# Three edits in one: a bias matmul over 128 rows instead of 3, the second layer norm's statistics on ScalarE, a cast written as a maximum

## The reference, cut to what matters

```python
x = x + linear_attention(layernorm(x)) @ W_proj + b_proj   # 16 heads of 8, causal running sums
z = layernorm(x)                    # (x - mean) / sqrt(var + 1e-5), over 128 channels
logits = z @ Wr + br                # 8 experts
# the two best experts of each token, their softmax weights normed to sum 1
h = relu(z @ W1[e] + b1[e])         # 512 wide
y_e = h @ W2[e] + b2[e]
x = x + sum of weight_e * y_e over the token's two experts
```

## Time and profile before

| | us |
|---|---|
| median of 3 runs | 402.93 (401.96 to 403.1) |
| the profiled execution, time | 401.86 |
| the same, span of the profile | 400.1 |
| PE busy | 311.0 (78%) |
| DVE busy | 297.5 (74%) |
| POOL busy | 280.4 (70%) |
| ACT busy | 193.4 (48%) |
| mean granted TensorE clock | 0.894 of full speed |

### The profile page before, as it was taken

The page is one execution under the profiler, slowest core; times in us unless marked ns, Lnnn a source line. Parts: engine busy times, 40 slices in busy tenths (PEclk is TensorE's granted clock), DMA queues, the critical chain, the costliest instruction groups (busy, mean ns, idle before and its releaser), DMA issues.

```text
span 400.1 us, 8377 instructions
## 1 busy us (share of the span) xinstructions
PE 311.0 (78%) x2477; PEld 241.8 (60%) x2477; DVE 297.5 (74%) x702; ACT 193.4 (48%) x480; POOL 280.4 (70%) x251
## 2 busy tenths in 40 slices
PE   5899999696979959889841389998999999993000
PEld 4678766464646636666530368887888888882000
DVE  6898998996779898799963777766666667773067
ACT  2788216557223210533312256776677777771072
POOL 3869376899457887887765636878788788787500
PEclk9999999899899987999955569999999999998555
DMA  7970000000000100000110142312423233111198
GB/s 221 346 221 1 2 0 0 2 2 0 2 0 20 35 28 20 27 22 27 41 48 33 47 128 70 81 56 87 115 83 83 83 91 89 43 43 52 46 374 256
DMA packets 23958, 29.26 MB, mean 73 GB/s; under 512 B 3806, under 2 KB 18569, under 8 KB 23916
## 3 DMA queue, kind: packets, MB, share of 16 engines
q1 hardware_dynamic: 18934, 19.02, 15.9%
q0 software_dynamic: 4544, 9.38, 7.3%
q10 hardware_dynamic: 438, 0.33, 0.3%
HBM read 16.04 MB, written 12.67 MB: 72 GB/s over the span
## 4 chain that ended last, share of the span: by engine, by line
PE 32%; DVE 23%; issue 19%; POOL 13%; ACT 9%; DMA 3%; SPq 0%; POOLq 0%; DVEq 0%; ACTq 0%
POOL y_rows L514 9%; PE ps L1191 7%; DVE work L845 4%; PE ps L1190 3%; DVE nd L851 3%; POOL x_rows L479 3%; DVE y_s L862 3%; PE ps L1162 2%; PE ps L1392 2%; ACT xs L610 2%; DVE x L1123 2%; PE ps L1362 2%; PE ps L1393 2%; PE ps L1364 2%; PE ps L1363 2%
## 5 line engine op out<-in xcount | busy, mean ns | idle before, releaser
L514 POOL DMA_INDIRECT y_rows<-kvt,yid x78 | 95.5, 1225 | 30.3 <-issue 21.0
L479 POOL DMA_INDIRECT x_rows<-rows,pos_i x64 | 66.1, 1034 | 30.2 <-issue 17.3
L449 POOL TENSOR_TENSOR kvt<-qk,v 128x1024 f32<-128x1024 f32 x32 | 67.6, 2136 | 24.4 <-PE ps L1195 13.2
L1191 PE MATMUL ps<-kvt,tri 128*128 128x384 f32 (+1 forms) x192 | 70.2, 477 | 12.1 <-DVE work L845 12.1
L676 ACT ACTIVATE wraw<-ps,b1s 128x256 f32<-128x256 f32 x156 | 61.3, 475 | 2.8 <-PE ps L1364 2.5
L1191 PEld LDWEIGHTS ps<-kvt,tri 128*128 128x128 f32 x192 | 37.0, 200 | 33.0 <-issue 16.5
L1071 DVE CAST wraw<-wraw 128x1024 f16<-128x1024 f32 x39 | 27.2, 696 | 34.7 <-ACT wraw L676 33.4
L1075 DVE TENSOR_TENSOR wraw<-wraw 128x1024 f16<-128x1024 f32 x39 | 47.8, 1226 | 1.3
L845 DVE TENSOR_TENSOR work<-ps,qk 128x1152 f32<-128x1152 f32 x32 | 42.2, 1351 | 3.5 <-PE ps L1195 3.2
L1362 PE MATMUL ps<-wraw,w1h 128*128 128x256 f16 x156 | 43.4, 278 | 0.3 <-issue 0.3
L1363 PE MATMUL ps<-wraw,w1h 128*128 128x256 f16 x156 | 43.3, 278 | 0.0
(11 more groups left out here) (211 smaller groups left out, 650.0 us busy)
## 6 DMA issues: line engine op xcount, KB each, us to landing
wraw<-x_rows SPq DMA_DIRECT2D x39, 130.0 KB, 2.6
qk<-y_rows SPq DMA_DIRECT2D x8, 512.0 KB, 6.6
wraw<-in_L_ffn_W_dram SPq DMA_DIRECT2D x1, 2048.0 KB, 11.8
out_dram<-x SPq DMA_DIRECT2D x8, 256.0 KB, 4.5
x<-in_L_attn_x_dram SPq DMA_DIRECT2D x3, 512.0 KB, 7.9
y_rows<-kvt,yid POOLq DMA_INDIRECT x78, 2.5
x_rows<-empty SPq DMA_DIRECT2D x9, 130.0 KB, 3.1
x_rows<-rows,pos_i POOLq DMA_INDIRECT x64, 2.3
```

The source lines that it names most:

```text
L449: nc.gpsimd.tensor_tensor(kvt[:, u % RING, a].rearrange("p (j h i) -> p j h i", j=DH, i=DH), k.unsqueeze(1).broadcast_to([P, DH, H, DH]), ...
L479: nc.gpsimd.indirect_dma_start(out=x_rows, out_offset=bass.IndirectOffsetOnAxis(ap=pos_i[:, c, t:t + 1], axis=0), in_=rows[:, t, :], in_of ...
L514: nc.gpsimd.indirect_dma_start(out=y_rows, in_=ysb[:, n % YG, g], in_offset=None, out_offset=bass.IndirectOffsetOnAxis(ap=yid[:, n, g:g + ...
L1191: nc.tensor.matmul(o, tri[:, :], kv[a][:, cols], start=(a == 0), stop=True)
```

## The change

The bias matmul of the experts' output reads 128 rows: the tile b2p has 128 partitions, set to zero on GpSimd, of which the first three take the pieces; the weights are the 128x128 ones that the first stage has already. `copy_x2` on ScalarE becomes two activations that also give each row's sum. A new `statistics` on ScalarE, for unit s - 1 and between `copy_yT(s)` and `copy_x2(s)`, turns the sums into negative means and takes squares of x minus mean with their sum (the squares themselves go to a place that is written again later). GpSimd's `layer_norm_2` gets one more small operation, which turns the sum of squares into the variance. VectorE's `statistics` and `moments_2` go. The high half is the maximum of the fp32 tile with itself, written in fp16.

```diff
-        b2p = sb("b2p", [3, E, D], BF16)
-        ones3 = sb("ones3", [3, P], BF16)
+        b2p = sb("b2p", [P, E, D], BF16)
@@ SP
+            sp.wait_ge(late_done, 16)
-            sp.dma_start(b2p[:, :, :], b2_parts).then_inc(b2_in, 16)
+            sp.dma_start(b2p[0:3, :, :], b2_parts).then_inc(b2_in, 16)
@@ GpSimd
-            nc.gpsimd.memset(ones3[:], 1.0).then_inc(late_done, 1)
+            nc.gpsimd.memset(b2p[:, :, :], 0.0).then_inc(late_done, 1)
@@ layer_norm_2(g), GpSimd
-                pool.wait_ge(stats2_done, g + 1)
-                nc.gpsimd.tensor_tensor(rstd[:, 1, gt], lnt[:, 4, gt], neghalf[:, gt], ALU.pow).then_inc(rstd2_done, 1)
+                pool.wait_ge(squares_done, G_LAST[g] + 1)
+                nc.gpsimd.tensor_scalar(var[:, gt], squares[:, gt], 1.0 / (D * X_SCALE ** 2), LN_EPS / X_SCALE ** 2, ALU.mult,
+                                        ALU.add).then_inc(var_done, 1)
+                pool.wait_ge(var_done, g + 1)
+                nc.gpsimd.tensor_tensor(rstd[:, 1, gt], var[:, gt], neghalf[:, gt], ALU.pow).then_inc(rstd2_done, 1)
@@ ScalarE
             def copy_x2(u):
                 act.wait_ge(proj_done, u + 1)
-                nc.scalar.activation(tiles(x, u), ps[:, 7, 0:T].rearrange("p (a d) -> p a d", a=TPU), ACT.Copy).then_inc(x2_done, 1)
+                for a in range(TPU):
+                    t = u * TPU + a
+                    ins = nc.scalar.activation(x[:, t], ps[:, 7, a * P:(a + 1) * P], ACT.Copy, accum_out=sums[:, t:t + 1])
+                ins.then_inc(x2_done, 1)
+            def statistics(u):
+                act.wait_ge(x2_done, u + 1)
+                nc.scalar.activation(tiles(mean, u), tiles(sums, u), ACT.Copy, scale=-1.0 / D).then_inc(mean_done, 1)
+                act.wait_ge(mean_done, u + 1)
+                for a in range(TPU):
+                    t = u * TPU + a
+                    ins = nc.scalar.activation(rows[:, t, 0:D], x[:, t], ACT.Square, bias=mean[:, t:t + 1],
+                                               accum_out=squares[:, t:t + 1])
+                ins.then_inc(squares_done, 1)
@@ ScalarE, step s
                 copy_yT(s)
+                if s >= 1:
+                    statistics(s - 1)
                 copy_x2(s)
@@ VectorE, step s
-                if s >= 1:
-                    statistics(s - 1)
...
-                if s - 1 in ended_by:
-                    moments_2(ended_by[s - 1])
@@ hidden_high(n), VectorE
-                nc.vector.tensor_copy(hh[:, n % 2], hid[:, n % 2]).then_inc(hi_done, 1)
+                nc.vector.tensor_tensor(hh[:, n % 2], hid[:, n % 2], hid[:, n % 2], ALU.max).then_inc(hi_done, 1)
@@ down(n), TensorE
-                nc.tensor.matmul(both, ones3[:, :], b2p[:, bass.ds(e, 1), :].broadcast_to([3, GPB, D]), start=True, stop=False)
+                nc.tensor.matmul(both, ones_b[:, :], b2p[:, bass.ds(e, 1), :].broadcast_to([P, GPB, D]), start=True, stop=False)
```

More of the change, by code:

```diff
@@ L145, in block_kernel @@
         lnt = sb("lnt", [P, 7, NT])
+        sums = sb("sums", [P, NT])
+        mean = sb("mean", [P, NT])
+        squares = sb("squares", [P, NT])
+        var = sb("var", [P, NT])
         rstd = sb("rstd", [P, 2, NT])
@@ L258, in block_kernel @@
         x2_done = sem("x2_done")
-        bn2_done = sem("bn2_done")
-        stats2_done = sem("stats2_done")
+        mean_done = sem("mean_done")
+        squares_done = sem("squares_done")
+        var_done = sem("var_done")
         rstd2_done = sem("rstd2_done")
@@ L466, in layer_norm_2 @@
                 gt = tiles_of(g)
-                pool.wait_ge(stats2_done, g + 1)
-                nc.gpsimd.tensor_tensor(rstd[:, 1, gt], lnt[:, 4, gt], neghalf[:, gt], ALU.pow).then_inc(rstd2_done, 1)
+                pool.wait_ge(squares_done, G_LAST[g] + 1)
[3 more added lines that the diff above has]
+                nc.gpsimd.tensor_tensor(rstd[:, 1, gt], var[:, gt], neghalf[:, gt], ALU.pow).then_inc(rstd2_done, 1)
                 pool.wait_ge(rstd2_done, g + 1)
-                nc.gpsimd.tensor_tensor(shift[:, 1, gt], lnt[:, 3, gt], rstd[:, 1, gt], ALU.mult).then_inc(shift2_done, 1)
+                nc.gpsimd.tensor_tensor(shift[:, 1, gt], mean[:, gt], rstd[:, 1, gt], ALU.mult).then_inc(shift2_done, 1)
             def scatter_x(n):
@@ L647, in _ @@
                     norm_2(ended_by[s - 2])
+            statistics(U - 1)
             for g in (NG - 2, NG - 1):
@@ L863, in quotient @@
                                         rd[:, par].unsqueeze(2).broadcast_to([P, TPU, DH, H]), ALU.mult).then_inc(y_done, 1)
[L865 to L875, removed]
             def split_low(g):
@@ L1035, in foreign_slots @@
                 link(nc.vector.tensor_tensor(aside[:, :, :], outside[:, 0], spare[:, :, :], ALU.mult))
-            statistics(U - 1)
-            moments_2(NG - 1)
             choose(FIRST)
```

## The result

The changed kernel took 398.0 us (median of 12 runs, 396.45 to 399.42) against 402.81 for the kernel before (12 runs, 400.38 to 403.4): ratio 0.9888, 95% interval 0.9866 to 0.991. The forecast was 398.6. The profiled execution took 398.36 us, span 396.6, mean granted clock 0.889.

What follows compares the result with a forecast made beforehand. No single engine was taken to decide; in the expert blocks TensorE sets the pace, then a fixed tail. The terms -4.4 + 0 - 4.7 + 4.5 + 0.3 = -4.3 gave 397.6 us profiled, 398.6 as median, range 395.5 to 402.

Steps and rivals of the forecast that it cites:

- Part 1: Expert blocks: bias matmul over 128 rows saves 0.20 us a block on TensorE, -4.4 us (0 to -5.5).
- rival A: Bias matmul: the chip sees no gap from its rows, so -4.4 goes and time is 403.0 us; chance 0.13.
- a fixed tail: End of the expert blocks: after VectorE's last subtract frees GpSimd, what remains was taken as fixed.
- Part 2: Expert blocks: the cast as a maximum adds 0.53 us a block on VectorE but costs 0 (-1 to +2).
- Rivals C and D: Scatters: C, two-input operations don't hold them, 387.7 us, chance 0.05; D, GpSimd can't get between maximum and subtract, 428, 0.03.
- covered: Blocks 1 to 6: VectorE is some 1.5 us late in total, but the stall of block 12 hides it.
- Part 3: Attention steps: statistics moved to ScalarE; VectorE -4.7, ScalarE +4.5, GpSimd's extra operation +0.3 us.
- ScalarE's term: Attention: +0.9 us from yT copy to next denominator, counting in steps 2, 4, 5, 6 and 11: +4.5 us.
- Rival B: Attention: a sum output costs 0.4 and nothing overlaps, 2.15 us a step instead of 0.9; 407.3 us; chance 0.11.
- VectorE's relief: Attention: VectorE loses two bn_stats per step and seven small operations per group, -4.7 us (-2 to -6).
- the four terms of 0.95: Attention steps 6, 9, 11 and 13: VectorE's small group operations leave the path before the next multiply, 4 x 0.95 us.
- the bounds of part 3: Attention: VectorE's saving -2 to -6 us, ScalarE's cost +1.8 to +8.5; named as the source of the forecast's range.

Runs made afterwards that it cites:

- the 64 rows: Kernel before with only the bias matmul changed, to 64 rows instead of 3, on a chip where the kernel before takes 401.83 us: 400.84 us, ratio 0.9984.

## Why the prediction was right, point by point

**Part 1, -4.4: right in mechanism; right in size partly by luck, since the sum of it is made up otherwise.** The gap was 0.20 a block as predicted and went in full; rival A is refuted by the bias alone and by the 64 rows. But blocks came to 3.03, not 2.99. PE in one of the longer blocks of the changed kernel:

```profile
291.28 0.22 PE L1399 MATMUL ps<-w,wraw 128*128 x1
291.34 0.22 PE L1400 MATMUL ps<-w,wraw 128*128 x1
291.46 0.23 PE L1399 MATMUL ps<-w,wraw 128*128 x1
291.58 0.23 PE L1400 MATMUL ps<-w,wraw 128*128 x1
291.64 0.22 PE L1399 MATMUL ps<-w,wraw 128*128 x1
```

Two of the 16 high matmuls come 0.12 apart instead of 0.055. Their row took 0.90 on the mean before and 0.94 after (means over blocks 14 to 35); the bias alone has the same 0.94 with the cast kept, so it is not the maximum. Some blocks have it and some don't (2.99 and 3.1). It is the same row that grew on the 420 us chips, from 1.03 to 1.22. Its cause is open. 21 periods thus gave 21 x 0.16 = 3.3 us. The rest came from where I had put "a fixed tail". POOL after:

```profile
360.68 0.96 POOL L522 DMA_INDIRECT y_rows<-kvt,yid  x1 [0.31 <-issue]
361.95 0.96 POOL L522 DMA_INDIRECT y_rows<-kvt,yid  x1 [0.30 <-issue]
...
373.31 0.96 POOL L522 DMA_INDIRECT y_rows<-kvt,yid  x1 [0.30 <-issue]
```

The last copy starts at 361.80, with 10 scatters still to start; before it was 11 (363.93 to 376.72). Counted by their starts, GpSimd stood 10 scatters behind ScalarE's copies in blocks 18 to 33 before, and 9 after (10 in a few blocks): it keeps VectorE's pace of two a block, as predicted, with one less in hand. That is 1.3 us more, with the bias alone too (11.5 us from the last copy to the last scatter, against 12.8 before). Between the bias of block 35 and the last copy 0.3 is lost again. From the bias of block 14 to the last scatter: 89.6 us before, 85.4 after, -4.2. Nothing in the prediction foresaw that one scatter, and without it this part would have been -3.

**Part 2, 0: right.** Timelines of DVE and POOL in the changed kernel:

```profile
291.99 1.23 DVE L1078 TENSOR_TENSOR wraw<-wraw 128x1024 f16<-128x1024 f32 x1 [0.19 <-ACT wraw L701]
293.25 1.22 DVE L1082 TENSOR_TENSOR wraw<-wraw 128x1024 f16<-128x1024 f32 x1
```

```profile
291.35 0.96 POOL L522 DMA_INDIRECT y_rows<-kvt,yid  x1 [0.30 <-issue]
292.61 1.44 POOL L522 DMA_INDIRECT y_rows<-kvt,yid  x1 [0.30 <-issue]
294.35 0.96 POOL L522 DMA_INDIRECT y_rows<-kvt,yid  x1 [0.30 <-issue]
```

The scatter of 292.61 starts inside the maximum (291.99 to 293.22) and ends at 294.05, 0.96 from 0.13 before the maximum's end: it got in ahead of the subtract, which starts only 0.03 later. Rivals C and D are both out. One detail was wrong: not both scatters of a block are lengthened, only that in the maximum; the next one comes when the subtract is over anyway. The Trainium skill (SBUF — State Buffer, section Who interferes with whom) infers that a two-input operation leaves GpSimd's descriptor writing alone; the trace disagrees with that inference, at 292.61 as at 317.93 in the earlier trace rows. VectorE, at 2.85 a block, is still idle ahead of 31 of the 39 maxima, and of every one from block 13 on (10.3 us in all, 9.5 of it a wait for ScalarE). One place of cost was missed: in block 0 the copy of the group counts, which the bias matmul of block 0 waits for, is queued behind the subtract. From the last yT copy to bias 0 it was 32.2 to 32.7 us in the five kernels with the cast and no statistics, 33.1 to 33.3 in the four with the maximum: +0.7 where I wrote that it is covered. By block 14 nothing of it is left (from bias 0 to bias 14 it was 47.4 us in the bias alone and 45.9 with the maximum).

**Part 3, -4.7 + 4.5 + 0.3 = +0.1: the net is about right, both big terms were too large, ScalarE's by far.** ScalarE's term was mis-sized. Its timeline in attention step 10 after:

```profile
159.64 0.38 ACT L603 ACTIVATE xT_s<-ps 128x256 f32<-128x256 f32 x1 [4.51 <-PE ps L1209]
159.92 0.20 ACT L615 ACTIVATE mean<-sums 128x2 f32<-128x2 f32 x1
160.15 0.40 ACT L619 ACTIVATE rows<-x,mean 128x128 f32<-128x128 f32 x1
160.46 0.19 ACT L619 ACTIVATION_READ_ACCUMULATOR rows<-x,mean 128x1 f32 x1
160.55 0.39 ACT L619 ACTIVATE rows<-x,mean 128x128 f32<-128x128 f32 x1
160.84 0.19 ACT L619 ACTIVATION_READ_ACCUMULATOR rows<-x,mean 128x1 f32 x1
160.93 0.25 ACT L609 ACTIVATE x<-ps 128x128 f32<-128x128 f32 x1
...
165.84 0.32 ACT L596 ACTIVATE rd<-nd,den_eps 128x32 f32<-128x32 f32 x1
```

From the yT copy to the next denominator 6.20 us, against 158.77 to 164.64 = 5.87 before: +0.33, the low bound of 0.35 and not 0.9. A square comes 0.40 after the other (I took 0.5), the whole statistics fit the wait for the projection but for 0.10, and the two copies with sums take 0.50 where one of 256 took 0.28. Rival B needed 1.75. Five steps make 1.7 us, not 4.5.

VectorE's relief in front of the multiplies is there. From the quotient's end to the next multiply in steps 6, 9, 11 and 13: 4.04, 4.29, 1.72, 2.11 before; 3.15, 3.21, 0.83, 1.17 after: 3.8 us, as the four terms of 0.95 said. The bn_stats gave nothing: the reciprocals wait for the denominator all the same, 24.9 us in 16 instead of 12.7 in 7.

By these two, attention should have ended 2 us earlier. It did not. The last yT copy starts at 208.5 (207.5 before), and over all kernels with the statistics at 206.3 to 208.5, mean 207.5 of five, over the nine without at 205.8 to 208.9, mean 207.5. One reason is that one end of one execution can't show it: steps of unchanged code differ by more. Windows of TensorE's clock (columns as in the earlier trace rows) of the changed kernel and of the one with 64 rows:

```profile
90.00:105.00 15.00, 10.34 (x33) 6.54 (x32) 8.91 (x12) 9.82 (x29) 10.73 (x10) 0.73 0.00 1
```

```profile
90.00:105.00 15.00, 11.02 (x59) 7.97 (x57) 10.43 (x15) 8.24 (x20) 11.44 (x10) 1.00 0.00 0
```

From the yT copy of step 4 to that of step 5 it was 17.1 us in the first, at a granted clock of 0.73 of full speed, and 13.7 in the second, at full speed throughout; the kernel before had 15.4 at 0.89, the bias alone 16.4 at 0.77. TensorE runs part of this stretch at 1.2 GHz instead of 2.4 and the stage follows.

The steps around this stretch hardly scatter, so stretches can be compared over all profiles, from the first multiply of one step to that of another (us; clock is the granted one from 92 to 118 us):

| | steps 0 to 4 | steps 5, 6 | clock there | steps 7 to 14 |
|---|---|---|---|---|
| before | 45.88 | 25.82 | 0.93 | 80.19 |
| 64 rows | 45.91 | 24.12 | 1.00 | 80.29 |
| bias; bias and maximum (third chip) | 44.71; 44.72 | 27.31; 27.46 | 0.87 | 80.35; 80.45 |
| five without statistics (420 us chips) | 45.84 to 45.89 | 25.60 to 25.84 | 0.93 | 80.09 to 80.24 |
| whole change | 47.01 | 27.02 | 0.80 | 78.97 |
| statistics in front of `copy_yT` | 45.93 | 26.31 | 0.87 | 78.80 |
| three with statistics (420 us chips) | 46.99 | 25.61; 24.49; 24.47 | 0.87; 0.93; 0.93 | 78.73 to 78.98 |

The statistics cost 1.1 us in steps 0 to 4, and nothing there when they stand in front of `copy_yT`: that is ScalarE's time ahead of the denominator, put at 0.9 in each of steps 2 and 4, and it fits the 1.0 us between the ratios of these two kernels. (The 44.7 of the third chip goes with a granted clock of 1.00 from 46 to 84 us, where all the others have 0.96.) They give back 1.4 us in steps 7 to 14, and in steps 5 and 6 1.0 to 1.9 where the clock is the same. At equal clock they are thus worth -1.3 to -2.2 in attention, as the two terms had it; but the profiled execution of the whole change had the lowest clock of all in steps 5 and 6 and lost it again. Whether the statistics, which shift what TensorE waits for, make such stretches more frequent these single executions don't tell. Behind attention they cost 0.5 on a 402 us chip (from the last yT copy to bias 0: 33.5 against 33.1 for bias and maximum; but 32.8 with the statistics in front of `copy_yT`, so this much one execution doesn't settle). GpSimd's variance operation behaved as predicted: 216.64, in front of the power at 216.93, +0.3.

**Together.** From bias 14 on -4.2; before it +0.8 (287.12 to 287.95); after the last scatter -0.1: -3.5 in the two profiled executions, -4.8 in the medians. The forecast was right because its first term carried it alone, and that term landed near -4.4 with the help of one scatter that it didn't count. The others cancelled each other as forecast, but at other sizes, and how far each counts depends on the clock of the execution. The forecast's own range of 395.5 to 402 is not what the bounds of part 3 give: with -6 and +1.8 the sum comes to 394.6, with -2 and +8.5 to 405.3.

## What to carry to other kernels

A matmul of few rows among full ones cost 0.20 us here on top of its own 0.11; so where the load of a short matmul shows idle time that no other engine ends, and TensorE sets the pace, pad its constant tile with zeros to 128 rows, and look whether the time comes back as idle elsewhere, as it did on two of the chips. Price work that is moved to ScalarE from start to start of neighbouring rows, since its small operations overlap, and count nothing for relief where the relieved engine waits for another anyway. Time the parts of a change separately: here one of three carried all of the gain. Where a stage's clock moves, compare stretches of many profiles and not the ends of two.

## What the runs showed of the hardware

- 3 rows and 64 rows next to 128-row matmuls: 0.20 to 0.21 us from start to start on both sides; 128 rows: 0.11. The load takes 91, 92 and 98 ns.
- A two-input operation of 1024 fp32 elements on VectorE holds the start of GpSimd's indirect DMA until 0.13 us before its end, and GpSimd gets in between two such operations that follow each other within 0.03 us. A scatter that began before the operation is not held.
- A sum output of an activation is a separate record of 0.19 us, and the next instruction starts 0.09 after it.
- The same program takes 402 us on some chips and 420 on others. For the bias alone the whole difference lies behind bias 0: 5.6 to 12.8 us for three of the first seven blocks, and later 3.61 us a block instead of 3.03 at the full granted clock, less 9.5 of a shorter tail. On the second kind the change costs 2.9 us instead of saving 4.8.
